# Second small-head layer of a cross-attention kernel: divisions and spreads two steps apart, one exponential over two banks

## The reference, cut to what matters

```python
x = L0(x, ctx)        # two cross-attentions, 16 heads of 128, an extra bias key, then an MLP
x = L1(x, ctx, mask)  # cross-attention, 16 heads of 16, then an MLP
x = L2(ctx, x, mask)  # "second small-head layer"
x = L3(x, ctx, mask)  # 32 heads of 8 over 8 key heads, then a layer norm

def L2(x, latents, attention_mask):          # x is ctx, latents is the running x
    h = concatenate([x, latents], axis=1)    # 512 keys
    q = (latents @ q_w + q_b).reshape(b, 256, 16, 16)
    k, v = split((h @ kv_w + kv_b).reshape(b, 512, 16, 16, 2))
    attn = softmax(where(full_mask, einsum('bkhd,bnhd->bhkn', q, k) / 16, -inf))
    out = einsum('bhkn,bnhd->bkhd', attn, v) @ out_w + out_b + latents
    return gelu(rmsnorm(out) @ mlp_w1 + mlp_b1) @ mlp_w2 + mlp_b2 + latents
```

## Time and profile before

| | before |
|---|---|
| median of 3 runs | 1274.03 us |
| profiled execution, its own time | 1277.74 us |
| its span, first to last instruction | 1276.3 us |
| TensorE matmuls busy | 1226.1 us, 96% |
| TensorE weight loads busy | 1035.4 us, 81% |
| DVE, ScalarE, POOL busy | 70%, 61%, 47% |
| mean granted TensorE clock | 0.991 |
| exponentials L2159, all three small-head layers | x320, 176.6 us, 594 ns each |
| `Q<-rows` DMAs of layer 2 | 62, landing after 2.0 us in the median |

### The profile page before, as it was taken

One profiled execution on the slowest core, in us unless ns is written; L12 is line 12 of the kernel. 1 busy time (PEld: TensorE's weight loads), 2 busy tenths in 40 slices (PEclk: granted clock), 3 DMA queues, 4 the chain that ended last, 5 costly groups with the idle time before them and its releaser, 6 DMA issues. The chain is left out here.

```text
span 1276.3 us, 27220 instructions
## 1 busy us (share of the span) xinstructions
PE 1226.1 (96%) x9979; PEld 1035.4 (81%) x9979; DVE 890.4 (70%) x2304; ACT 782.2 (61%) x1889; POOL 598.9 (47%) x966
## 2 busy tenths in 40 slices
PE   8999999999999999999999999899998889999997
PEld 7999999999999999999988555785665578666664
DVE  5887777779877777878855775537767564767664
ACT  4876666668866666666864655646665654455553
POOL 3784545548765554546832432404433231334333
PEclk9999999999999999999999999999989899999999
DMA  5441001114421001002401310122413012221100
GB/s 172 148 138 34 27 26 35 30 34 127 138 77 34 26 26 34 26 26 70 128 25 44 105 53 3 50 76 86 75 36 83 2 54 68 59 67 36 46 12 18
DMA packets 56820, 75.03 MB, mean 59 GB/s; under 512 B 11312, under 2 KB 30576, under 8 KB 56688
## 3 DMA queue, kind: packets, MB, share of 16 engines
q1 hardware_dynamic: 51568, 72.75, 19.2%
q0 software_dynamic: 5120, 0.56, 0.3%
HBM read 49.46 MB, written 1.05 MB: 40 GB/s over the span
## 5 line engine op out<-in xcount | busy, mean ns | idle before, releaser
L1095 POOL TENSOR_SCALAR E<-E,rl 128x256 f32<-128x256 f32 x256 | 243.1, 960 | 211.0 <-DVE rl L980 211.0
L2159 ACT ACTIVATE PT<-bank 128x512 f32<-128x512 f32 x320 | 176.6, 594 | 115.8 <-PE bank L2001 58.9
L846 ACT ACTIVATE QTh<-bank,bqs 128x256 fp32r<-128x256 f32 x128 | 60.7, 474 | 156.3 <-PE bank L127 156.2
L2242 DVE CUSTOM_DVE_ANT_0 Em<-bank,M 128x256 bf16<-128x256 f32 x256 | 95.1, 419 | 53.8 <-PE bank L1987 22.3
L856 ACT ACTIVATE E<-bank,nm 128x257 f32<-128x257 f32 x256 | 119.3, 480 | 1.2 <-DVE nm L950 1.1
L2236 DVE TENSOR_REDUCE nm<-bank 128x1 f32<-128x512 f32 x128 | 83.9, 684 | 41.7 <-PE bank L1983 40.7
L2001 PE MATMUL bank<-Q,K 51*128 51x256 f32 (+1 forms) x640 | 103.4, 323 | 6.1 <-DMA Q<-rows 4.5
L984 DVE TENSOR_TENSOR PTl<-bank,PTh 128x512 fp32r<-128x512 f32 x128 | 87.9, 687 | 27.7 <-ACT PTh L868 27.3
L957 DVE SCALAR_TENSOR_TENSOR QTl<-bank,bqs,QTh 128x256 fp32r<-128x256 f32 x128 | 61.5, 481 | 63.7 <-ACT KT L847 62.9
L2290 POOL DMA_DIRECT2D Q<-rows x96 | 54.2, 566 | 107.4 <-ACT rows L2173 107.4
L868 ACT CAST PTh<-bank 128x512 fp32r<-128x512 f32 x128 | 75.2, 587 | 43.6 <-PE bank L771 43.6
(11 more groups left out here) (438 smaller groups left out, 4423.6 us busy)
## 6 DMA issues: line engine op xcount, KB each, us to landing
stage<-in_wts SPq DMA_DIRECT2D x99, 256.0 KB, 3.2
U<-in_vrows SPq DMA_DIRECT2D x64, 256.0 KB, 2.7
K<-stage SPq DMA_DIRECT2D x48, 128.0 KB
Q<-stage SPq DMA_DIRECT2D x48, 128.0 KB
K<-stage SPq DMA_DIRECT2D x48, 64.0 KB
Q<-stage SPq DMA_DIRECT2D x48, 64.0 KB
K<-xh SPq DMA_DIRECT2D x16, 128.0 KB, 3.2
Q<-rows POOLq DMA_DIRECT2D x96, 4.0 KB, 1.9
```

The costliest lines, as they stand in the source:

```text
L1095: m = pool.tensor_scalar(s.E[:, i % 3, t, 0:256], s.E[:, i % 3, t, 0:256], s.rl[:, r, t:t + 1], None, ALU.mult)
L2159: act.activation(s.PT[i % s.NPT][:, 2 * u:2 * u + 2, :].rearrange("p a b -> p (a b)"), s.STB[y][:], ACT.Exp).then_inc(S["t_ex"])
L2242: dve.tensor_tensor_reduce(out=s.Em[:, (2 * i + e) % 4], in0=bank[:, e * 256:e * 256 + 256], in1=s.M3[:, j, e, :], scale=-1.0, scalar=3.4e ...
```

## The change

It does five things, all for layer 2.

- `po0` and `on0` stand one step earlier (key 4), so that the two divisions are two steps apart.
- In the preparation, `q_out` goes from step 8 to 6, `k_out` from 9 to 8, and the projection of x with its parts from 7 to 8. `q_out` thereby stands ahead of `mask_out` in SP's order. The spreads are then at 6, 8 and 10.
- One exponential covers both heads of a step: its input is the two banks `STB` as one (1024 columns), its output two head tiles. It waits for all four key matmuls, and `t_ex` rises by 2 at its end.
- For that the `PT` tiles are allocated in pairs, and layer 2 keeps 6 instead of 7 of them; the eight PSUM banks become one tensor.
- `OS` becomes two tiles instead of one with two halves.

```diff
-KEPT = {1: 8, 2: 7, 3: 6}
+KEPT = {1: 8, 2: 6, 3: 6}
...
-                4: ["q0", "q1", "qh", "ql", "maskrow"], 6: ["k0", "k1", "kh", "kl"], 7: ["x0", "x1", "xh", "xl"],
-                8: ["mask_out", "q_out"], 9: ["k_out"], 10: ["v0", "v1", "va", "x_out"]},
+                4: ["q0", "q1", "qh", "ql", "maskrow"], 6: ["k0", "k1", "kh", "kl", "q_out"],
+                8: ["x0", "x1", "xh", "xl", "mask_out", "k_out"], 10: ["v0", "v1", "va", "x_out"]},
...
-         2: {5: ["po0", "on0"], 6: ["po1", "on1"], 8: ["onT", "oth", "otl"], 13: ["c0", "c1", "y"]},
+         2: {4: ["po0", "on0"], 6: ["po1", "on1"], 8: ["onT", "oth", "otl"], 13: ["c0", "c1", "y"]},
...
-        self.PT = [sb("PT", [128, self.nkt, 256]) for _ in range(self.NPT)]
+        self.PTs = [sb("PT", [128, 2, self.nkt, 256]) for _ in range(self.NPT // 2)]
+        self.PT = [self.PTs[k // 2][:, k % 2] for k in range(self.NPT)]
...
-        self.OS = sb("OS", [128, 2, self.nh // 4, 256])
+        self.OS = [sb("OS", [128, self.nh // 4, 256]) for _ in range(2)]
...
+    def exps_of_pair(n):
+
+        p, u, y = s.unit(n)
+        w.wait_ge(S["t_st"], s.o["st"] + n + 2)
+        w.wait_ge(S["t_pv"], s.o["pv"] + (2 * p + 1 - s.NPT) // 4 + 1)
+        act.activation(s.PTs[p % (s.NPT // 2)][:, :, 2 * u:2 * u + 2, :].rearrange("p h a b -> p h (a b)"), c.banks[:, 3:5, :], ACT.Exp
+                       ).then_inc(S["t_ex"], 2)
...
         for k in s.in_step(n - s.L):
-            exps(k)
+            if l != 2:
+                exps(k)
+            elif k % 2 == 0:
+                exps_of_pair(k)
...
-        c.B = [top.enter_context(nc.psum_tensor(f"bank{i}", [128, 512], F32)) for i in range(8)]
+        c.banks = top.enter_context(nc.psum_tensor("bank", [128, 8, 512], F32))
+        c.B = [c.banks[:, i, :] for i in range(8)]
```

More of the change, by code:

```diff
@@ L1737, in heads_post_pe @@
         for g in range(4):
-            z = pe.transpose(s.MB[:, g * 128:g * 128 + 128], s.OS[:, j, 4 * u + g, t * 128:t * 128 + 128], c.ident[:])
+            z = pe.transpose(s.MB[:, g * 128:g * 128 + 128], s.OS[j][:, 4 * u + g, t * 128:t * 128 + 128], c.ident[:])
         z.then_inc(S["h_po"])
@@ L1828, in close_pe @@
         for g in range(4):
-            z = pe.transpose(bank[:, g * 128:g * 128 + 128], s.OS[:, 1, 4 + g, t * 128:t * 128 + 128], c.ident[:])
+            z = pe.transpose(bank[:, g * 128:g * 128 + 128], s.OS[1][:, 4 + g, t * 128:t * 128 + 128], c.ident[:])
         z.then_inc(S["h_po"])
@@ L2166, in attended @@
             w.wait_ge(S["h_po"], s.po(b - 1, 0))
-        act.copy(s.OS[:, j, g, :], s.OB[:, 0:256]).then_inc(S["t_os"])
+        act.copy(s.OS[j][:, g, :], s.OB[:, 0:256]).then_inc(S["t_os"])
     def maxima_rows(g):
```

## The result

The kernel after takes 1269.58 us in the median of 10 runs (1265.82 to 1271.9), the kernel before 1273.96 us in the median of 10 beside them (1271.58 to 1278.85): 0.9953 of the time, 95% interval 0.9938 to 0.9969. This ratio, here and in the experiments, is the comparison's own estimate and not the quotient of the two medians, which is 0.9966 here; gains in us with an interval behind them are worked out from the ratio. It was timed again later (last experiment): 1268.0 us and once more 0.9953 (0.9934 to 0.9971). The gain is real and lies at the edge of what the prediction called no change.

What follows compares the result with a forecast made beforehand. TensorE, busy 96% of the span, was taken as the bound, with its idle and half-clock time to win. From 1277.74 us, -3.7 -3.9 -0.9 +2.7 -0.6 gave 1271.3 (1267.7 to 1275, 45%; 8 in 10: 1263.5 to 1280).

Steps and rivals of the forecast that it cites:

- Spreads: SP's queue in layer 2: an earlier stream cuts TensorE's waits for the maxima rows' DMA, -3.7 us (bounds -4.3 and 0).
- the 4 us that the prediction named as a sign of being wrong: Row DMAs in the new profile still landing after 4 us or more would show the prediction wrong.
- Clock: TensorE after the two row waits: most of the half-clock time comes back, -3.9 us (bounds -4.8 and 0).
- Divisions: Batch passages: po1's wait goes, the turn waits for np instead, -0.9 us over three (bounds -3.0 and +1.3).
- Exponential: ScalarE loop: one 1024-column exponential costs +0.11 us in about 25 gated steps, +2.7 us (bounds -1.3 and +8).
- the signs named beforehand: In the new profile: exponentials of 1.0 to 1.05 us, key matmuls waiting for PT over 17 times, about 0.3 us each.
- x later: Steps 8 and 9: xh on ScalarE comes behind no attend's input, -0.6 us over three batches (bounds -1 and +1).
- that the DMA wait isn't cured: Late rows come from packets slow in themselves or weight loads collide elsewhere; 1278.9 or 1275.2 us; 20% chance.
- That the exponential's loop becomes the bound: TensorE waits for 1024 columns at each step's first key matmul; 1281.7 us; 10% chance.
- That it takes 1.19 us: The two-bank exponential lasts as long as two of 594 ns, +4 us over 25 gated steps, 1275.6 us; within forecast's upper edge.
- All the low clock gone: No idle in the three passages lowers TensorE's clock; 1263.3 us, or 1264.7 with the exponential's cost halved; 25% chance.

Runs made afterwards that it cites:

- last experiment: The changed kernel timed once more with no edit: 1268.0 us, 0.9953 of the kernel before.
- x later alone: The kernel before with only x's projection and parts moved from step 7 to 8, spreads left where they were: 1272.3 us, 0.9986.
- Q first alone: The kernel before with only q_out moved from step 8 to 6, ahead of mask_out in SP's queue: 1267.50 us, 0.9945.
- Q first with the statistics: The kernel before with q_out at step 6 ahead of mask_out and the next MLP's second-batch norm statistics one step earlier: 1267.87 us, 0.9956.
- the weight loads later: The kernel before with SP holding the fourth batch's four weight loads until the key matmuls of that batch's step 1: 1273.18 us, 0.9987.

## Why the prediction was right, point by point

Forecast 1271.3, measured 1269.58: in the forecast's own range (1267.7 to 1275) and, at 0.47%, just within the 0.5% given the most chance. Its gain from the profiled execution was 6.4 us; measured are 4.4 between the medians of the first comparison, 5.5 between the means of all runs, 6.0 by the ratio. How the terms did:

1. *Spreads, -3.7 us for the waits: right in size, the reason shown for the fourth batch only.* The wait of the third batch is gone; 0.76 us is left in the fourth, where 0.5 was kept, and that fits the reason given there (weight loads at 954.44 beside the rows of an earlier step). For the third batch the prediction's reason was that the rows would meet only the tail of a stream that ends 3.4 us earlier. That isn't shown: x later alone removes the same wait with the stream in its old place. Waits for the rows fell by 3.7 us, 4.5 to 0.8. SP's Q spread started at 904.88 instead of 910.89, of which 1.4 us is the layer's own earlier start. The Trainium skill, "DMA: Bandwidth & Descriptors", section "Queues, rings and completion order", states that each DMA engine goes round the queue rows packet by packet. The prediction concluded from it that a small transfer never waits out a backlog, by which the term was near 0. The runs disagree with a term near 0: with the mask ahead of Q rows landed after up to 6.1 us, with Q first after at most 4.5 (3.9 in after, just under the 4 us that the prediction named as a sign of being wrong). What the page states of the engines is neither shown nor refuted here, as slow packets could delay the rows without a backlog. The small number of waits was a weak objection; two were enough.
2. *Clock, -3.9: right in kind, its size only bounded.* Both stretches behind the two waits are gone. The prediction had each stretch begin just after an idle; the first began inside it, at about 925.0, while TensorE waited until 926.0 (windows of the kernel before; TensorE's busy time stands second, the clock third from the end):

```profile
924.50:925.00 0.50, 0.00 (x0) 0.00 (x0) 0.47 (x2) 0.00 (x0) 0.50 (x1) 1.00 1.13 117
925.00:925.50 0.50, 0.00 (x0) 0.00 (x0) 0.50 (x2) 0.00 (x0) 0.03 (x1) 0.54 1.11 193
```

   10.0 us at half clock lower the mean by 0.0039 (10.0/1276/2), which by the slopes above is worth 3.1 to 3.5 us. Terms 1 and 2 together were 7.6 us. Q first alone has them and little else: 7.0 us (4.5 to 9.6). In after, with everything else, it is 5.5.
3. *Divisions, -0.9: nothing measurable, 0.9998 (-2.2 to +1.7 us).* The wait changed its name as forecast, from `On` to `np`. It was 0.26 us in the third batch, shorter than the 0.5 to 0.9 expected. What the step left out: with late rows, a TensorE that comes earlier waits longer for them (2.23 to 2.83 us). A gain of 0.9 us is within the interval, so it is not refuted either.
4. *Exponential, +2.7: right alone, probably too large in the sum.* Length 1021 ns (estimate 1.02). In the step after 900.48 the next one begins at 902.19, 0.68 us after the first's end (0.64 to 0.70 forecast), 1.71 us apart instead of 1.54. Timeline of ScalarE and of the key loads:

```profile
900.48 1.03 ACT L2168 ACTIVATE PT<-bank 128x1024 f32<-128x1024 f32 x1
...
901.56 0.30 PEld L2002 LDWEIGHTS bank<-Q,K 51*128 51x128 f32 x4 [0.52 <-ACT PT L2168]
...
902.19 1.03 ACT L2168 ACTIVATE PT<-bank 128x1024 f32<-128x1024 f32 x1 [0.68 <-PE bank L2002]
```

   On the old order it costs +2.2 us, as forecast. In the new one, two pairs of kernels (after without it and after; Q first with the statistics, without and with it) show 0.9962 against 0.9953 and 0.9956 against 0.9955: zero, give or take 2 us; the fitted lines at equal clock give +0.7 and +1.5. What was mis-sized is the product of about 25 gated steps and 0.11 us; which of the two isn't shown. Of the signs named beforehand one came differently: the weight loads waited for `PT` 14 times, not more often than 17, but longer (8.0 us against 4.8), and the matmuls 19 times for 0.2 us each (4.3 by 19).
5. *x later, -0.6:* 0.9986, -1.8 us (-3.3 to -0.3) on the old order. Right in sign, but the reason was another: it took the third batch's wait away. Beside Q first there is nothing left of it (0.9953 for all spreads, 0.9945 for Q alone).

So three terms missed: +2.7 for the exponential and -0.9 and -0.6 for divisions and x are all near zero or small in the final order, and they offset each other but for 1.2 us. The fourth error is the basis. The sum was set on the profiled execution, 3.4 us above the mean of all runs of before (1277.74 less 1274.3), with the remark that a part of the surplus was probably the first DMA wait itself. That isn't borne out: the late rows of the third batch are also in the profiles of the exponential alone (1.74 us), the divisions alone (2.83) and the weight loads later (1.89), so they are regular. Its mean clock of 0.991 is only 0.001 below the average and by the slopes explains less than 1 us; the rest of the surplus stays unexplained.

The forecast lay 1.7 us above the first median and 2.5 above the mean of all runs of after. That it came so close is partly luck. Basis and small terms put it 3.4 and 1.2 us too high, and terms 1 and 2, at 7.6 us, took off 2.1 us more than the 5.5 that the whole change gained.

The rivals: that the DMA wait isn't cured (20%) is refuted by waits and landings. But the cause that this rival named, packets slow in themselves, fits the third batch better than the backlog does (last section). That the exponential's loop becomes the bound (10%) is refuted by the two pairs. That it takes 1.19 us fell with 1021 ns. All the low clock gone (25%): one stretch stayed, behind a wait the change doesn't touch. The profiled execution of Q first alone shows that case: no stretch in the layer, 1264.27 us, beside the 1263.3 of this rival. Its four other runs have clocks of 0.993 to 0.996 and took 1267.3 to 1268.1 us.

## What stays open

Why the packets of the third batch are slow in some kernels, and so why moving x's projection cures its wait. Why Q first alone brings as much as the whole change and, at equal clock, 2 us more than it: the exponential's 0.7 to 1.5 us may be a part, the intervals overlap, and five rounds don't settle it. Why the half clock follows some waits of about 1 us and not others of the same length: `po1` waited 1.4 us three times in the Q-first kernel and no low stretch followed, while in Q first with the statistics one followed the same wait, and in after one followed a wait of 1.04 us. A way to hold the second norm's statistics off that place for good wasn't tried. No version is shown to beat the kernel after beyond its interval; the nearest is Q first alone, with one moved entry instead of five parts.

## What to carry to other kernels

A small late transfer can cost twice: its wait, and the half clock that comes with it; look for what the issuing queue sends in the same microseconds, and move the blocking entry (here a mask row whose data comes late) behind those that are ready. Test the parts of a bundled change singly: here one list entry out of five edits was enough for all of the gain. Before a sum is set on a profiled execution, compare its time and its mean clock with those of the other runs. And test a cause also where it should do harm: the stream issued later, and x moved with the stream in place, showed that the order of the queue works otherwise than thought.

## What the runs showed of the hardware

Around 920 us the same spreads took up to about twice the engines' time in some kernels. Windows of 918 to 920 us, first the kernel before, then x later alone (clock, DMA share and GB/s stand last):

```profile
918.00:920.00 2.00, 2.00 (x17) 1.35 (x15) 0.95 (x3) 0.95 (x4) 0.75 (x2) 1.00 1.18 152
```

```profile
918.00:920.00 2.00, 2.00 (x17) 1.27 (x14) 1.31 (x4) 1.33 (x3) 1.11 (x2) 1.00 0.73 195
```

A share of 1.18 for 152 GB/s against 0.73 for 195: packets lasted 2.1 times as long for the same bytes (1.18/152 by 0.73/195). The divisions alone (1.13, 173), the exponential alone (1.11, 170) and the weight loads later (1.05, 181) show it too. With the kernel before these are the four in which the third batch waits 1.7 us or more for its rows. All others have a share of 0.66 to 0.87 at 178 to 213 GB/s, as Q first (0.69, 190), and wait there 0.8 us or not at all. So in the third batch the slow packets go with the waits; that they cause them is likely but not shown, and their own cause wasn't found.
